# Splitting shift rows, q and k into high and low parts on GpSimd instead of ScalarE and VectorE, in an attention and mixture-of-experts kernel

## What is computed

```python
result = (embeddings @ w_qkv).reshape(b, s, 3, 16, 8)          # q, k, v
scores = einsum('bnqd,bnkd->bnqk', q, k) / sqrt(128)
out    = softmax(scores) @ v
x = layernorm(x + out)
# experts: sigmoid gates, top 8 of 16, normalised weights
y = sum_e combine_e * (silu(x Wg_e^T) * (x Wu_e^T)) Wd_e^T + shared expert
x = layernorm(x + y)
```

## Time and profile before

| what | value |
|---|---|
| median of 3 runs | 757.54 us (755.36 to 762.06) |
| the profiled execution, its own time | 760.73 us |
| its span, first to last instruction | 759.0 us |
| mean granted TensorE clock | 0.951 |
| attention block | first instruction to about 427 us of the span |
| PE, DVE, ACT, POOL busy in the span | 93%, 70%, 56%, 34% |

### The profile page before, as it was taken

One profiled execution on the slowest core, in us unless ns is written; L12 is line 12 of the kernel. 1 busy time (PEld: TensorE's weight loads), 2 busy tenths in 40 slices (PEclk: granted clock), 3 DMA queues, 4 the chain that ended last, 5 costly groups with the idle time before them and its releaser, 6 DMA issues. The chain is left out here.

```text
span 759.0 us, 13175 instructions
## 1 busy us (share of the span) xinstructions
PE 703.3 (93%) x3488; PEld 365.5 (48%) x3488; DVE 533.8 (70%) x1130; ACT 421.6 (56%) x824; POOL 258.7 (34%) x281
## 2 busy tenths in 40 slices
PE   2898999989999999999989999999999999999995
PEld 1333333333333333333333466767676766666663
DVE  1979999999999999999982264656566565646343
ACT  2067787877788787887775443424343333434321
POOL 2102101111011111111110275647566566566563
PEclk8569999999999999999995799999999999999999
DMA  5822241422414124141100505041331405050600
GB/s 178 264 77 86 80 119 63 133 66 79 139 53 126 64 75 147 45 148 65 38 4 2 223 1 207 18 174 63 106 130 57 180 16 221 5 232 0 238 1 28
DMA packets 34279, 74.89 MB, mean 99 GB/s; under 512 B 4144, under 2 KB 13488, under 8 KB 30032
## 3 DMA queue, kind: packets, MB, share of 16 engines
q1 hardware_dynamic: 33440, 72.38, 27.6%
q0 software_dynamic: 816, 2.23, 0.8%
HBM read 58.61 MB, written 15.99 MB: 98 GB/s over the span
## 5 line engine op out<-in xcount | busy, mean ns | idle before, releaser
L661 DVE TENSOR_REDUCE maxima<-ps_q 128x1 f32<-128x512 f32 x512 | 318.7, 682 | 36.7 <-PE ps_q L721 35.1
L618 ACT ACTIVATE probs<-ps_k 128x512 f32<-128x512 f32 x512 | 270.1, 609 | 96.2 <-PE ps_k L728 96.0
L943 POOL TENSOR_TENSOR hidden<-gated,weights 128x512 f32<-128x512 f32 x128 | 167.2, 1312 | 124.1 <-DVE gated L1025 107.9
L721 PE MATMUL ps_q<-k_aug,q_aug 32*128 32x512 f32 x512 | 179.8, 517 | 13.1 <-DMA q_aug<-q_rows 9.2
L728 PE MATMUL ps_k<-q_aug,k_aug 32*128 32x512 f32 x512 | 162.7, 499 | 25.6 <-ACT probs L618 23.6
L973 ACT ACTIVATE silu<-ps_gate 128x512 f32<-128x512 f32 x136 | 81.3, 598 | 176.9 <-PE ps_gate L1067 176.6
L1025 DVE TENSOR_TENSOR gated<-silu,ps_up 128x512 f32<-128x512 f32 x128 | 87.0, 685 | 106.9 <-PE ps_up L1067 71.6
L728 PEld LDWEIGHTS ps_k<-q_aug,k_aug 32*128 32x128 f32 x512 | 64.1, 189 | 182.2 <-ACT probs L618 154.7
L741 PE MATMUL ps_ctx<-probs,v_ones 128*32 128x512 f32 x1024 | 144.3, 638 | 0.0
L1092 PE MATMUL ps_y<-hidden,nets_down 128*128 128x512 f32 x272 | 137.1, 592 | 0.0
L1064 PE MATMUL ps_gate<-x1T_high,nets_low 128*128 128x512 f32 x136 | 96.6, 710 | 0.0
(11 more groups left out here) (93 smaller groups left out, 542.1 us busy)
## 6 DMA issues: line engine op xcount, KB each, us to landing
weights<-combine_rows SPq DMA_DIRECT2D x32, 1024.0 KB, 7.9
k_aug<-k_rows SPq DMA_DIRECT2D x32, 256.0 KB, 2.7
q_aug<-q_rows SPq DMA_DIRECT2D x32, 256.0 KB, 3.0
q_rows<-qk_high SPq DMA_DIRECT2D x16, 256.0 KB, 2.9
k_rows<-qk_high SPq DMA_DIRECT2D x16, 256.0 KB, 3.0
net_raw<-w_nets POOLq DMA_DIRECT2D x17, 128.0 KB, 3.4
xT_sb<-xT SPq DMA_DIRECT2D x8, 256.0 KB, 2.9
q_rows<-qk_low SPq DMA_DIRECT2D x8, 256.0 KB, 3.0
```

Source lines behind the costliest of these rows:

```text
L618: act.activation(probs[:, t % 2, h, :], ps_k[SCORE_SLOT[i]][:], ACT.Exp, scale=ATT_SCALE).then_inc(exp_done, 1)
L661: dve.tensor_reduce(maxima[:, parity, TILES * h + t:TILES * h + t + 1], ps_q[SCORE_SLOT[i % SCORES]][:], AX_X, ALU.max).then_inc(scores_q_ ...
L721: return pe.matmul(ps_q[SCORE_SLOT[i]][:], q_aug[rows, g, t * P:(t + 1) * P], k_aug[rows, g, :], start=True, stop=True).then_inc(scores_q, 1)
L943: pool.tensor_tensor(hidden[:, s % RING, :], gated[:, s % UP_RING, :], r.weights[:, e, :], ALU.mult).then_inc(hidden_done, 1)
```

## The change

In the loop ACT makes only one copy of the shift rows, of q and of k, the raw one (`stage_shift`, `stage_qk`), and announces it with new semaphores `shift_staged` and `qk_staged`. POOL makes the high part by multiplying the raw copy by ones into the float32r tile, and the low part by subtracting (`split_shift`, `split_qk`). DVE no longer does either in the loop. PE waits for the raw copy where it waited for the high part before it reuses `ps_turned`. The parts of unit 0 and batch 0, ahead of the loop, are made as before (`first_shift`, `first_qk`, `first_shift_low`, `first_qk_low`). In POOL's program `split_shift` and, in g = 0, both `split_qk` stand at the start of each unit, ahead of `place_v`, `add_context` and `split_net`.

```diff
@@ POOL
+            def split_shift(u):
+                pool.wait_ge(shift_staged, u + 1)
+                pool.wait_ge(shift_written, DMA * u)
+                pool.tensor_tensor(shift[:, 0, :], shift_raw[:], r.ones[0:GROUP * TILES, 0:P], ALU.mult
+                                   ).then_inc(shift_high, 1)
+                pool.wait_ge(shift_high, u + 1)
+                pool.tensor_tensor(shift[:, 1, :], shift_raw[:], shift[:, 0, :].bitcast(F32), ALU.subtract
+                                   ).then_inc(shift_split, 1)
+
+            def split_qk(b, i):
+                pool.wait_ge(qk_staged, 2 * b + i + 1)
+                pool.wait_ge(rows_written, 6 * DMA * b)
+                pool.tensor_tensor(qk_high[:, i, :], qk_raw[:, i, :], r.ones[:], ALU.mult
+                                   ).then_inc(qk_highs, 1)
+                pool.wait_ge(qk_highs, 2 * b + i + 1)
+                pool.tensor_tensor(qk_low[:, i, :], qk_raw[:, i, :], qk_high[:, i, :].bitcast(F32), ALU.subtract
+                                   ).then_inc(qk_split, 1)
...
             def body(b, first=False, last=False):
                 for g in range(GROUPS):
                     u = GROUPS * b + g
+                    if not (last and g == GROUPS - 1):
+                        split_shift(u + 1)
+                    if g == 0 and not last:
+                        split_qk(b + 1, 0)
+                        split_qk(b + 1, 1)
                     if not (first and g == 0) and not (last and g > 0):
@@ ACT
-            def round_shift(u, first):
+            def stage_shift(u, src):
                 act.wait_ge(maxima_turned, u + 1)
-                if not first:
-                    act.wait_ge(shift_loaded, GROUP * DMA * u)
-                act.copy(shift_raw[:], ps_misc[0:GROUP * TILES, 0:P])
-                act.copy(shift[:, 0, :], ps_misc[0:GROUP * TILES, 0:P]).then_inc(shift_high, 1)
+                act.wait_ge(shift_split, u)
+                act.copy(shift_raw[:], src[0:GROUP * TILES, 0:P]).then_inc(shift_staged, 1)
...
+            def stage_qk(b, i, src):
                 act.wait_ge(qk_projected, 2 * b + i + 1)
-                if not first:
-                    act.wait_ge(rows_written, 6 * DMA * b)
-                act.copy(qk_raw[:, i, :], src[:])
-                act.copy(qk_high[:, i, :], src[:]).then_inc(qk_highs, 1)
+                act.wait_ge(qk_split, 2 * (b - 1) + i + 1)
+                act.copy(qk_raw[:, i, :], src[:]).then_inc(qk_staged, 1)
@@ DVE
-                        if i == 3 and not (last and g == GROUPS - 1):
-                            split_shift(u + 1)
...
-                        if i == 9 and g == 0 and not last:
-                            split_qk(b + 1, 0)
-                        if i == 13 and g == 0 and not last:
-                            split_qk(b + 1, 1)
@@ PE
                             if (t, h) == (1, 2) and project:
-                                pe.wait_ge(shift_high, u + 2)
+                                pe.wait_ge(shift_staged, u + 2)
...
                             if (t, h) == (2, 2) and project:
-                                pe.wait_ge(qk_highs, 2 * b + 3)
+                                pe.wait_ge(qk_staged, 2 * b + 3)
...
                             if (t, h) == (3, 1) and project:
-                                pe.wait_ge(qk_highs, 2 * b + 4)
+                                pe.wait_ge(qk_staged, 2 * b + 4)
```

More of the change, by code:

```diff
@@ L400, in attention @@
         qk_projected = sem("qk_projected")
+        qk_staged = sem("qk_staged")
         qk_highs = sem("qk_highs")
@@ L410, in attention @@
         maxima_turned = sem("maxima_turned")
+        shift_staged = sem("shift_staged")
         shift_high = sem("shift_high")
@@ L586, in copy_context, with first_shift, first_qk @@
                 act.copy(c.context_T[:], ps_ctx[:]).then_inc(c.copied, 1)
-            def round_shift(u, first):
+            def stage_shift(u, src):
                 act.wait_ge(maxima_turned, u + 1)
-                if not first:
-                    act.wait_ge(shift_loaded, GROUP * DMA * u)
-                act.copy(shift_raw[:], ps_misc[0:GROUP * TILES, 0:P])
-                act.copy(shift[:, 0, :], ps_misc[0:GROUP * TILES, 0:P]).then_inc(shift_high, 1)
-            def round_qk(b, i, src, first):
-                act.wait_ge(qk_projected, 2 * b + i + 1)
-                if not first:
-                    act.wait_ge(rows_written, 6 * DMA * b)
-                act.copy(qk_raw[:, i, :], src[:])
+                act.wait_ge(shift_split, u)
+                act.copy(shift_raw[:], src[0:GROUP * TILES, 0:P]).then_inc(shift_staged, 1)
+            def first_shift(src):
+                act.wait_ge(maxima_turned, 1)
+                act.copy(shift_raw[:], src[0:GROUP * TILES, 0:P]).then_inc(shift_staged, 1)
+                act.copy(shift[:, 0, :], src[0:GROUP * TILES, 0:P]).then_inc(shift_high, 1)
+            def stage_qk(b, i, src):
+                act.wait_ge(qk_projected, 2 * b + i + 1)
+                act.wait_ge(qk_split, 2 * (b - 1) + i + 1)
+                act.copy(qk_raw[:, i, :], src[:]).then_inc(qk_staged, 1)
+            def first_qk(i, src):
+                act.wait_ge(qk_projected, i + 1)
+                act.copy(qk_raw[:, i, :], src[:]).then_inc(qk_staged, 1)
                 act.copy(qk_high[:, i, :], src[:]).then_inc(qk_highs, 1)
@@ L620, in body @@
                             if (t, h) == (0, 3) and not (last and g == GROUPS - 1):
-                                round_shift(u + 1, False)
+                                stage_shift(u + 1, ps_misc)
                             if (t, h) == (1, 0) and g == 0 and not first:
@@ L626, in body @@
                             if (t, h) == (1, 3) and g == 0 and not last:
-                                round_qk(b + 1, 0, ps_misc, False)
+                                stage_qk(b + 1, 0, ps_misc)
                             if (t, h) == (2, 3) and g == 0 and not last:
-                                round_qk(b + 1, 1, ps_misc, False)
+                                stage_qk(b + 1, 1, ps_misc)
                             if (g, t, h) == (2, 2, 1) and last:
@@ L641, in body @@
                                 stage_v(b + 1, ps_misc, False)
-            round_qk(0, 0, ps_misc, True)
-            round_qk(0, 1, ps_ctx, True)
+            first_qk(0, ps_misc)
+            first_qk(1, ps_ctx)
             stage_v(0, ps_k[0], True)
-            round_shift(0, True)
+            first_shift(ps_misc)
             body(0, first=True)
@@ L662, in take_maximum, with first_shift_low, first_qk_low @@
                                   AX_X, ALU.max).then_inc(scores_q_used, 1)
-            def split_shift(u):
-                dve.wait_ge(shift_high, u + 1)
+            def first_shift_low():
+                dve.wait_ge(shift_high, 1)
                 dve.tensor_tensor(shift[:, 1, :], shift_raw[:],
                                   shift[:, 0, :].bitcast(F32), ALU.subtract).then_inc(shift_split, 1)
-            def split_qk(b, i):
-                dve.wait_ge(qk_highs, 2 * b + i + 1)
+            def first_qk_low(i):
+                dve.wait_ge(qk_highs, i + 1)
                 dve.tensor_tensor(qk_low[:, i, :], qk_raw[:, i, :], qk_high[:, i, :].bitcast(F32),
@@ L701, in _ @@
             dve.memset(q_aug[:, 0, :].bitcast(F32), 0.0).then_inc(pads_set, 1)
-            split_qk(0, 0)
-            split_qk(0, 1)
+            first_qk_low(0)
+            first_qk_low(1)
             for u in range(AHEAD):
@@ L707, in _ @@
                 if u == 0:
-                    split_shift(0)
+                    first_shift_low()
             body(0, first=True)
@@ L811, in body @@
                                 else:
-                                    pe.wait_ge(shift_high, u + 1)
+                                    pe.wait_ge(shift_staged, u + 1)
                                 turn_maxima(u + 1, (g + 1) % 2)
                             if (t, h) == (3, 1) and project:
-                                pe.wait_ge(qk_highs, 2 * b + 4)
+                                pe.wait_ge(qk_staged, 2 * b + 4)
                                 project_v(ps_misc)
```

## The result

The changed kernel takes 777.45 us in the median of 4 runs (775.21 to 786.32); the kernel before, run beside it, 759.8 us (4 runs, 755.36 to 762.29). The ratio is 1.026, with an interval from 1.016 to 1.036. The interval is clear of 1, so the kernel is slower; whether by more or by less than 2% it doesn't settle. Between the medians lie 17.6 us where 14.7 were predicted, and since the interval spans 12 to 27 us, the two can't be told apart. The profiled execution is the longest of the four, 786.32 us, so its trace has more in it than a median run.

What follows compares the result with a forecast made beforehand. The bound was a PE-ACT round trip of 2.73 us per quad in attention. Gains -3.0, stall +4.5 and low clock +13.2 gave +14.7 on 757.5: 772 us, slower; range 760 to 783.

Steps and rivals of the forecast that it cites:

- The stall of unit 2: Batch 0: shift rows split late behind two nets, so PE stands still 3.9 to 5.2 us, taken as 4.5.
- The fall of the clock: At unit 2 of batch 0: PE's empty 4.5 us make the granted clock fall to 1.2 GHz.
- Its length: Low clock from unit 2 to unit 4's projections: ten quads, 1.39 us more each, 13.2 us after a deduction.
- rivals 3: After unit 2's stall, busy PE brings the clock back within two quads: 2.8 us, total 762; chance 0.14.
- Rival 1: Clock returns in unit 3, where PE turns the context: six quads, 8.3 us, total 767; chance 0.17.
- behind the second projection: Batch 0, kernel before: the clock rose at about 52.5 us, behind the second projection, after staying at 0.50 from 38.
- Rival 4: Batch 1's projections fail to lift the clock, low until unit 8: 22 quads, 30.6 us, about 788; chance 0.11.
- That sustained work ends the low clock: The skill's rule, by which the low clock ends soon after PE restarts; the forecast held 38 to 52 us against it.
- The work added on POOL in the loop at cost 0: Loop units: POOL has time for the added splits, and shift rows delayed behind a net still arrive in time: 0 us.
- that cover: Units after a net: shift rows land 0.6 to 1.9 us early; failing by 1 us would cost 12 us.
- The gains: Six batches: g = 3 quad 0.8 us, v's projection 1.8, k's projection 0.4; 3.0 us in all.
- rival 2: Not slower: removing DVE's subtractions shortens g = 0's projection quads, 11.5 us over seven batches, no stall: 746; chance 0.03.

Runs made afterwards that it cites:

- e1: Changed kernel with nets 0 and 1 put back ahead of the shift rows' split in g = 0 of batch 0: 762.38 us, ratio 1.004.
- e2: Changed kernel with v's placing in g = 0 ahead of the splits of q and k, nets still late: 765.78 us, ratio 1.011.
- e6: Kernel before, with only v's placing in g = 0 held back by a wait for k's low part and an idle multiplication: 765.52 us, ratio 1.007.
- e3: Changed kernel with nets 0 and 1 early in batch 0 and v's placing ahead of the q and k splits: 754.01 us, ratio 0.990.
- e5: As e3, but ACT makes the high parts by a second copy and PE waits for them; POOL only subtracts: 753.02 us, ratio 0.994.
- e8: The same kernel as e3, run on another chip: 749.68 us, ratio 0.990.
- e4: Changed kernel with four unused float32 matmuls on PE in the gap before unit 2: 775.36 us, ratio 1.020.
- e7: As e2, with four unused float32 matmuls on PE in the gap before unit 2: 760.13 us, ratio 1.000.

## Why the prediction was right, and where not

**The stall of unit 2: right.** Predicted 4.5 us, ended by a transfer from `shift_rows`; measured 4.67. The steps held as well: POOL's 128 x 512 took 1.27 to 1.28 us for the estimated 1.31, its 16 x 128 0.44 for 0.45. The nets came at 53.1, not 56, and all places lie about 3 us earlier, since in this execution the clock had risen before 48 us and not at 52.5. From the start of the first net's DMA (53.13) to the end of the second (63.48 + 0.73 = 64.21) passed 11.1 us for the 10.5 predicted.

**The fall of the clock: right. Its length: mis-sized.** The term was 13.2 us. In the trace the five quads from 63.27 to 87.97 took 24.70 us; e1, without gap, needs 13.81 for five such quads (60.21 to 74.02). The difference of 10.9 us is 4.7 for the stall and 6.2 for the clock. It came back in the first quad of unit 3, after four slow quads, and not with the projections of unit 4 after ten. That lies between rivals 3 (two quads) and 1 (six), and bears out the reason of neither. Rival 1 wanted the turning of the context, a full matmul, to bring it back; that turning came at 92.14, behind the rise, and the two turnings at 358.56 and 392.28 did not end the low clock there. Nor is it "behind the second projection" that it rises in batch 0, as the prediction read from the kernel before: in this trace it rose between 46 and 47 us, and the second projection began at 47.82. In e2 it was six quads and about 9 us. So 6 to 9 us, in place of 13.2: the price of a slow quad was about right (4.19 - 2.73 = 1.46 us for 1.39), their number was not. That 4.5 empty us would suffice for a fall was a guess that came true, since the earlier trace rows show only that 1.7 didn't. (Rival 4's own terms, 757.5 - 3.0 + 4.5 + 30.6, give 789.6 and not 788.)

**That sustained work ends the low clock: not here.** By the trace the clock stayed at 0.50 through the stretch from 362 to 400 us, with PE busy for 36.44 of 38 us. The Trainium skill ("TensorE: Matmul & The Clock Gate", Part 1: The HAM clock gate) has activity release the throttled state; in this stretch the trace doesn't agree. The same execution was back at full speed after some 18 us at unit 2 and after some 47 us there, so neither this rule nor my "the next projections bring it back" forecasts the length in this mix of matmuls.

**The work added on POOL in the loop at cost 0: this step failed.** I followed what the net delays (the shift rows in g = 2) and gave it 0.6 to 1.9 us to spare; that cover held, and PE waited for shift rows only once, at unit 2. What I did not follow is what now stands behind the two `split_qk` in g = 0: `place_v`, and through `v_placed` ACT's copy of the new v, the exponentials behind it and PE. This costs 0.78 us a batch, 4.7 us in six, by the trace; e6 reproduces it alone and e2 removes it. Worse is what it sets off: the clock falls behind such a quad in some batches. In the profiled execution, set against the same quads of the kernel before, these falls cost 2.4 us in batch 3 (206.26 to 217.44, 11.18 us for 8.77), 3.3 us in batch 5 (302.46 to 314.56, 12.10 for 8.78), and 15.5 us in batches 6 and 7, where twelve quads took 49.52 us (352.69 to 402.21) for 34.07.

**The gains: right in sum, partly by another quad.** v's projection gave 0.28 us a batch for the predicted 0.3, the g = 3 quad 0.14 as predicted, k's projection 0.17 where I had at most 0.1: 0.59 us a batch, 3.5 us in six, for the predicted 3.0. The batch did not shrink to 46.2 as said; it grew to 46.9 (112.43 to 159.33), by 0.78 - 0.59. e3, with the placing put right, has the 46.14. DVE's wait for PE grew from 19.2 to 52.0 us, as foreseen: 17.7 us of removed work turned into idle time, and the stall and slow quads account for more. e5 excludes rival 2, that DVE's relief shortens the projections.

**The sum.** Profiled execution: -3.5 (gains) + 4.7 (stall) + 6.2 (clock there) + 4.7 (placing) + 21.2 (falls behind it) = +33.3, of which 2.7 are given back by the earlier rise of the clock in batch 0. Measured between the two profiled executions is +25.6; the remaining 5.0 lie mostly where the kernel before itself ran at 0.50, from 398 to 424 us, and this execution for a shorter time, from about 435 us on (that attribution was read from the traces and not tested). The prediction's reason for that late fall, the end of the `score_q` tiles, is not borne out either: here they ended at 421.6 us and the clock stayed at 1.00 until 435. Between the medians it is 17.6: 12.1 for the four fixed terms; the other 5.5 are what is left for the falls and for the first and last batch, which vary by execution, and no run measures them alone. So +14.7 against +17.6 us is close by luck, by two errors of opposite sign: a clock term 4 to 7 us too large, and a term of about 10 us that was missing. Of the distance from 772 to 777.45 us another 2.3 come from the kernel before, whose median was 757.54 us when the forecast was made and 759.8 beside the changed kernel.

**What stays open.** e3 and e8 are 5.8 and 8.6 us below the kernel before in the median (7.7 each by the ratio), while the quads of six batches explain 3.5 and batch 0's projections half a microsecond more. The rest lies in the first and last batch, where the moments at which the clock rises and falls differ from execution to execution; no run separates this. Nor is it settled why the clock falls behind a long quad in some batches and not in others.

## What to carry to other kernels

When work is put on an engine that has time, list all that stands behind its new waits in that engine's program, and follow each item through its semaphores to the engine that sets the pace: twice here the trouble was the place in the line and not the work itself. The split of unit 2's shift rows stood behind two nets, the placing of v behind two splits, and moving the nets and the placing ahead again turned 2.6% slower into 1% faster. Where a delay on PE can't be avoided, price the clock behind it too: at unit 2 it cost 6 to 9 us for a delay of 4.7. And ask of a relief which wait it ends: DVE lost 17.7 us of work for nearly nothing, while a copy of ACT that PE waited for gave most of the gain.

## What was not expected of the hardware

- A quad longer by only 0.78 us (3.65 instead of 2.87), with PE idle for 1.01 us in it at most, was followed by a fall of the granted clock to 0.50: in 3 of 6 batches in e6 and in the changed kernel, 2 of 6 in e4, 1 of 6 in e1. That is 9 of 24; where this quad was 2.86 to 2.88 us (the kernel before, e2, e3, e5, e7, e8) it was none of 36.
- The time at 0.50 differed from 7 us (207 to 214) to 47 us (354 to 401) in one execution of one kernel, with PE 96% busy in the stretches measured in both: 5.74 of 6 us and 36.44 of 38.
- Four matmuls of float32 on a full tile in a gap of 5 us (the trace shows 3.70 us of them) kept the clock at 1.00, in both kernels that had them.
